# Moving ScalarE's entry work one batch later in the count matrix build of a graph network kernel

## The reference

```python
h = jnp.maximum(_layernorm(x), 0.0)
h = jnp.tanh(h @ W_in + b_in)                       # the entry
for _ in range(12):                                 # steps
    agg = segment_sum(h[src], dst) / deg
    h = h + (tanh(gelu(agg @ W1 + b1) @ W2 + b2) - decay * h) * 0.5
x = x + h
# then a layer norm and two graph convolutions, added to x
```

## Time and profile before

| what | value |
|---|---|
| median of 3 runs | 1358.31 us (1358.14 to 1360.56) |
| the profiled execution | 1362.37 us, of which its span is 1360.7 us |
| build of `adj`, last eviction begins | 137.04 us |
| TensorE busy in the span | 1276.2 us, 94% |
| VectorE, ScalarE busy | 392.7 us (29%), 323.7 us (24%) |
| mean granted TensorE clock | 0.981 of full speed |

### The profile page before, as it was taken

One profiled execution on the slowest core, in us unless ns is written; L12 is line 12 of the kernel. 1 busy time (PEld: TensorE's weight loads), 2 busy tenths in 40 slices (PEclk: granted clock), 3 DMA queues, 4 the chain that ended last, 5 costly groups with the idle time before them and its releaser, 6 DMA issues.

```text
span 1360.7 us, 17338 instructions
## 1 busy us (share of the span) xinstructions
PE 1276.2 (94%) x7201; PEld 712.6 (52%) x7201; DVE 392.7 (29%) x792; ACT 323.7 (24%) x474; POOL 45.2 (3%) x48
## 2 busy tenths in 40 slices
PE   2875999999999999999999999999999999979998
PEld 1764356455564555545545556455554554545545
DVE  6899013113121131221311312113112131451312
ACT  1788113113121131221311312113112121330100
POOL 3900000000000000000000000000000000000000
PEclk7899999999999999999999999999999999979999
DMA  3000200000000000000000000000000001120101
GB/s 95 1 1 0 61 1 0 0 0 0 0 0 0 0 0 0 0 0 0 0 0 0 0 0 0 0 0 0 0 0 0 0 0 39 47 57 0 47 17 33
DMA packets 24541, 13.66 MB, mean 10 GB/s; under 512 B 6171, under 2 KB 23605, under 8 KB 24384
## 3 DMA queue, kind: packets, MB, share of 16 engines
q1 hardware_dynamic: 22414, 12.28, 3.5%
q10 hardware_dynamic: 1698, 0.66, 0.2%
q0 software_dynamic: 400, 0.33, 0.1%
HBM read 9.42 MB, written 3.44 MB: 9 GB/s over the span
## 4 chain that ended last, share of the span: by engine, by line
PE 86%; DVE 7%; issue 3%; ACT 2%; DMA 2%; DVEq 0%; ACTq 0%; SPq 0%; POOL 0%; POOLq 0%
PE ps L630 34%; PE ps L632 32%; PE ps L653 10%; PE ps L644 8%; DVE scratch L996 4%; ACT scratch L787 1%; PE ps L557 1%; PE ps L680 1%; DVE ps L1102 1%; DMA adj<-packed_scratch,adj 1%; ACT adj L755 1%; DMA dinv_scratch<-cols 1%; DVE lo L979 0%; DMA adj<-adj 0%; PE ps L520 0%
## 5 line engine op out<-in xcount | busy, mean ns | idle before, releaser
L630 PE MATMUL ps<-adj,hi 128*128 128x512 f16 (+2 forms) x2450 | 814.5, 353 | 9.3 <-DVE lo L979 5.8
L632 PE MATMUL ps<-adj,lo 128*128 128x512 f16 (+2 forms) x2352 | 796.2, 353 | 0.0
L630 PEld LDWEIGHTS ps<-adj,hi 128*128 128x128 f16 x2450 | 238.3, 97 | 260.2 <-issue 21.8
L632 PEld LDWEIGHTS ps<-adj,lo 128*128 128x128 f16 x2352 | 229.3, 98 | 242.9 <-issue 23.0
L1102 DVE TENSOR_TENSOR ps<-ps,bias 128x512 f32<-128x512 f32 (+1 forms) x84 | 53.8, 641 | 538.0 <-PE ps L653 538.0
L795 ACT ACTIVATE scratch<-ps 128x512 f32<-128x512 f32 (+1 forms) x84 | 46.3, 551 | 644.8 <-DVE ps L1102 644.8
L644 PE MATMUL ps<-scratch,w 128*128 128x512 f32 (+2 forms) x336 | 141.5, 544 | 18.3 <-ACT scratch L787 18.3
L787 ACT ACTIVATE scratch<-ps,b1c,cols 128x512 f32<-128x512 f32 (+2 forms) x168 | 113.4, 722 | 159.7 <-PE ps L644 158.9
L653 PEld LDWEIGHTS ps<-w,scratch 128*128 128x128 f32 x1200 | 145.0, 194 | 6.3
L653 PE MATMUL ps<-w,scratch 128*128 128x128 f32 x1200 | 147.7, 277 | 0.0
L1095 DVE TENSOR_TENSOR scratch<-ps,scratch 128x512 f32<-128x512 f32 (+2 forms) x84 | 52.0, 619 | 187.6 <-PE ps L644 132.2
(11 more groups left out here) (129 smaller groups left out, 210.1 us busy)
## 6 DMA issues: line engine op xcount, KB each, us to landing
scratch<-rdeg_scratch SPq DMA_DIRECT2D x1, 1562.5 KB
state<-in_x_dram SPq DMA_DIRECT2D x5, 256.0 KB, 4.1
scratch<-in_x_dram SPq DMA_DIRECT2D x5, 256.0 KB, 2.8
x_scratch<-state SPq DMA_DIRECT2D x5, 256.0 KB, 2.8
scratch<-dinv_scratch SPq DMA_DIRECT2D x5, 256.0 KB, 3.8
state<-x_scratch SPq DMA_DIRECT2D x5, 256.0 KB, 4.1
out_dram<-state SPq DMA_DIRECT2D x5, 256.0 KB
adj<-adj SPq DMA_DIRECT2D x1, 390.6 KB, 4.0
```

What stands on the lines that cost most here:

```text
L630: nc.tensor.matmul(bank, hi[:, k, :], adj[:, k, c0:c0 + n], start=(at == 0), stop=False)
L632: mm = nc.tensor.matmul(bank, lo[:, k, :], adj[:, k, c0:c0 + n], start=False, stop=(k == K_ORDER[-1][0]))
```

## The change

ScalarE issues the copy, and the tanh with its hi, one batch later in its own order. Before, they stood behind the eviction of the batch at which TensorE issues the transpose or the product; now they stand behind the eviction after that. The order on TensorE and on VectorE is unchanged, and so is every instruction.

```diff
             for b in range(ENTRY_BATCHES):
                 evict(b % 2, b // 2)
-                if b in TURN_AT:
-                    entry_copy(TURN_AT.index(b))
-                if b in PROD_AT:
-                    entry_tanh(PROD_AT.index(b))
-                    split_hi(PROD_AT.index(b), PROD_AT.index(b) + 1, first_scale)
+                if b - 1 in TURN_AT:
+                    entry_copy(TURN_AT.index(b - 1))
+                if b - 1 in PROD_AT:
+                    entry_tanh(PROD_AT.index(b - 1))
+                    split_hi(PROD_AT.index(b - 1), PROD_AT.index(b - 1) + 1, first_scale)
```

## The result

The changed kernel takes 1374.58 us (median of 4 runs, 1374.1 to 1375.28), the kernel before 1358.66 (4 runs, 1358.14 to 1360.56): ratio 1.0115, 95% interval 1.0097 to 1.0133, so +15.9 us where 8.1 were forecast. (A fourth run of before has joined the three behind the table, so its median is 1358.66 and not 1358.31.) The sign and the place were right, the size lay outside the range.

The account below looks back on a forecast made before the run. VectorE bounds the build's groups before; afterwards a TensorE-ScalarE ring of 9.17 us instead of 7.70 does. Shift 6.9 us plus 1.2 for the clock is 8.1, so 1358.31 + 8.1 = 1366.4 us, range 1362.5 to 1371.

Parts of the forecast that it names:

- The ring: Build's entry groups: TensorE and ScalarE wait on each other from product to product, 9.17 us a group; chance as costed 0.74.
- The clock: Build's entry groups: two stretches of 3 to 4 us at granted clock 0.50 add 1.2 us, at most 4.0.
- the table load: Group 0: the tanh's table load, before begun while the product ran, now adds 1.28 us ahead of product 1.
- the short copy: Last entry group: its copy is shorter, estimated to take 0.3 us off.
- the upper bound: Each lowered-clock stretch falling wholly on TensorE's part costs half its length, up to 2.0 us; two give 4.0.
- product 0: Entry product of group 0: it waits for the later copy and starts at 46.91 instead of 46.54 us.
- the clock falls with the ring: Rival: TensorE idles more in the entry groups, so the lower clock holds longer; up to 1384 us, chance 0.12.
- Its milder form: Lower clock covers TensorE's part in one to three entry groups, 3.1 us each: 1369.5 to 1375.7 us.
- The tanh's alone: Moving only tanh and hi one batch later makes an entry group 7.81 us, over VectorE's 7.54.
- No change: Rival: VectorE, full in every build group and its instructions unmoved, remains the bound; 1358.3 us, chance 0.05.
- faster: Rival: ScalarE no longer idles before the tanh, products fall to VectorE's pace; 2.7 us gained at most, 1355.6, chance 0.05.
- given back: Rival: at the step's start up to 1.3 us of idle and some more won back; 1362 to 1365, chance 0.04.

Follow-up runs that it names:

- e6_fill3: Changed kernel plus useless TensorE products in each group: 15 before batch 4+4g's multiply, 12 before the entry product, 5 before batch 7+4g's multiply; 1367.61 us, ratio 1.0057.
- e2_tanh: Kernel before with only ScalarE's tanh and hi one batch later, the copy in its old place; 1368.83 us, ratio 1.0067 to the kernel before.
- e5_product: Changed kernel with TensorE's entry product also one batch later, behind the multiply of batch 5+4g; 1368.95 us, ratio 1.0068 to the kernel before.
- e1_copy: Kernel before with only ScalarE's copy one batch later, tanh and hi in their old place; 1364.05 us, ratio 1.0032 to the kernel before.
- The fillers: Useless TensorE products put in its gaps, results overwritten: 1369.09 and 1367.61 us on the changed kernel, 1360.46 us on the kernel before.
- e4_before_fill: Kernel before plus 20 useless TensorE products a group, before batch 4+4g's multiply and before the entry product; 1360.46 us, ratio 1.0003.

## Why the prediction was wrong

**The ring: right.** "2.04 + 1.05 + 1.36 + 1.26 + 2.72 + 0.59 + 0.15 = 9.17" measured 9.09 in every full group at full clock behind the first, in three kernels. Idle times forecast and measured: before the product 0.8 and 0.79, ScalarE before its eviction 1.9 and 1.80, VectorE 1.6 and 1.46. The shift by the ring alone was put at 6.9 and measured as 7.5 (e6_fill3; 7.3 by the profiles).

**The clock: the step that failed.** "If two such stretches of 3 to 4 us come again ... 0.6 each on the mean: +1.2" was the term. From product 0 to product 6 the changed kernel takes 109.04 - 45.79 = 63.25 us. Six bare rings of 9.09, the table load of 1.28 and 0.3 less for the short copy make 55.5. The other 7.7 us are the lower clock, in four of six rings. Three assumptions of that term went wrong. The number of stretches was taken over from before as if it came from outside the kernel; it doubled. Their length was taken over too, 3 to 4 us; three of the four lasted 6.8 us, most of a ring. And their place was averaged over the ring, of which TensorE has a third; in the changed kernel the three long ones begin 0.3 to 0.45 us behind a product's start and so cover nearly all of TensorE's part. The one in product 0's ring cost 1.2, the three others 2.1 to 2.25 each, more than the 2.0 that the upper bound allowed for one. With 7.7 in place of 1.2 the same sum gives 6.9 + 7.7 = 14.6, inside the measured interval of 13.2 to 18.1 us.

The place is not a rule: in e2_tanh a long stretch begins at 72.4 us and the product only at 73.98, in e5_product at 82.4 and 84.05. Why the stretches of the changed kernel begin where they do is open, and so is why e1_copy, whose ring is also longer than before, has only short ones.

A smaller miss is hidden by the traces' different starts. The prediction put product 0 0.37 us later than before. It came 0.75 us earlier on the profile's clock, but 1.48 later from the first eviction (8.32 us instead of 6.84). Part of that is the clock again: it was at 0.50 at the first eviction and rises to 1.00 at 43.9 us, 6.4 us behind the first eviction, where before it rose after 3.6 us (43.3). In e6_fill3 it rises after 2.2 us, and product 0 comes 0.80 later than before. Put together, the forecast's 6.9, 7.7 for the clock, 1.1 for product 0, 0.5 less for the shorter rings and 0.3 more behind product 6 make the 15.5 us of the traces. So most of the miss is the lower clock.

**The rival that held half the truth** was "the clock falls with the ring", with a chance of 0.12. Its milder form, one to three rings caught whole, gave 1369.5 to 1375.7 us, and the measured 1374.58 lies in it. That is luck in part: its top counts three rings at 3.1 us each where they cost 2.1 to 2.25, and it leaves out the fourth, of 1.2. It was argued down with the loop without entry work, emptier and at a clock of 1.00. That comparison was too coarse: it set mean busy shares of two different patterns of work against each other. The fillers are the test that the row could not be. They change nothing but TensorE's gaps, and the lowered stretches between product 0 and the loop went from four to two to none in the changed kernel, and from two to none in the kernel before (e4_before_fill). The Trainium skill ("TensorE: Matmul & The Clock Gate", Part 1) says that the clock follows how busy TensorE has been recently; the filler runs agree, and the prediction was wrong to set it aside. Why the loop without entry work, where TensorE is emptier than in any of these rings, mostly keeps its clock (the changed kernel has one lowered stretch there, at 119.5) is not settled here.

**The halves.** "The tanh's alone ... 7.81" missed an edge, through the multiply of batch 8+4g, and measured 8.25. It didn't enter the forecast, since in the full ring that edge is hidden.

**No change, faster, given back:** none happened. VectorE had the highest share of the three in the build before the change and does the same work in the same time after it, and still the build is 15.5 us longer. The Trainium skill ("Perfetto Trace Analysis", Identifying the Most-Contended Engine) says to work on the engine with the highest occupancy; read as a forecast of no change, that failed here. The shift at the build's end (13.58) reached step 1 (14.16) in full.

## What to carry to other kernels

Where engines hand work to each other in fixed orders, moving an instruction one place later in one engine's order can cost time even when no instruction is added and the busiest engine's order stays. Close the ring of waits that it lies on, add its terms, and compare the sum with the busiest engine's need. If the new ring makes TensorE wait, price the clock as a term that the change itself moves. In this kernel it was as large as the ring's own cost. Don't take the number or the length of the lowered stretches over from the trace before. A few useless products in TensorE's gaps are a cheap experiment that tells a ring's cost from the clock's.

## What the runs showed of the hardware that was not expected

Lowered stretches of 6.8 us began at 78.1 and 98.6 us in the changed kernel, where TensorE's idle gaps in the group before were no longer than 1.3 us (0.69, 1.27 and 0.79), and made the group 11.28 us instead of 9.09, the last one 10.87. Ahead of the one at 57.6 there was a gap of 2.69 us. With useless products in the gaps (e6_fill3) the granted clock was 1.00 from 42 to 140 us. In the kernel before, 20 of them a group made an undisturbed group 0.45 us longer (8.15 instead of 7.70) and the kernel no slower clear of noise. The price of a lowered stretch goes by what it covers: 6.8 us of it cost 2.1 to 2.25 here, where ScalarE's part of the ring ran on at its own pace.
